# Transposing x in blocks of 16 rows by two neighbouring columns instead of whole columns

## The reference, cut to what matters

```python
def _L0_conv_ref(x, p1, p3, p4, p5, p6):
    t1 = jnp.einsum('nchw,he->ncew', x, p1)            # p1: (32, 16), sums over the rows h
    t2 = three row-shifted copies of x
    t3 = conv(t1, p3, 9x9, one filter per channel)
    t4 = conv(t3, p4, 5x1, groups of 4 channels)
    t5 = jnp.einsum('ncew,ewf->ncf', t4, p5[:, :, 0, :])
    t6 = conv(t5, p6, 3 taps along f)
    return einsum('ncf,nfp->ncp', t6, t2) / sqrt(3 * c)
...
    x = x + _L0_conv_ref(_gn(x), ...)
    x = x + _L1_conv_ref(_gn(x), conv_w, gamma, beta)
```

## Time and profile before

| | us |
|---|---|
| median of 3 runs | 307.37 |
| lowest and highest | 307.35, 309.02 |
| the profiled execution | 308.8 |
| its span | 307.0 |

### The profile page before, as it was taken

The page is one execution under the profiler, slowest core; times in us unless marked ns, Lnnn a source line. Parts: engine busy times, 40 slices in busy tenths (PEclk is TensorE's granted clock), DMA queues, the critical chain, the costliest instruction groups (busy, mean ns, idle before and its releaser), DMA issues.

```text
span 307.0 us, 6666 instructions
## 1 busy us (share of the span) xinstructions
PE 251.1 (82%) x2662; PEld 192.6 (63%) x2662; DVE 237.2 (77%) x479; ACT 200.8 (65%) x268; POOL 164.5 (54%) x186
## 2 busy tenths in 40 slices
PE   6899978998775599899999999999999998850000
PEld 3333345665645397789998899888998887630000
DVE  2899996044564767778999999998999987866992
ACT  1788722277539254764878778787787777465990
POOL 4000001987605721578888898888988889540000
PEclk9999999999969599999999999999999999995555
DMA  7996041666710700000000000000000000000798
GB/s 218 410 410 227 0 125 38 177 179 173 235 63 2 275 0 0 2 0 2 1 0 2 1 0 0 3 0 2 0 0 2 2 0 3 0 0 20 316 403 355
DMA packets 11487, 28.00 MB, mean 91 GB/s; under 512 B 2528, under 2 KB 3616, under 8 KB 11456
## 3 DMA queue, kind: packets, MB, share of 16 engines
q1 hardware_dynamic: 8624, 21.37, 19.3%
q10 hardware_dynamic: 1232, 4.46, 3.9%
q0 software_dynamic: 1600, 1.74, 2.3%
HBM read 16.39 MB, written 8.39 MB: 81 GB/s over the span
## 4 chain that ended last, share of the span: by engine, by line
PE 70%; DVE 10%; issue 6%; POOL 4%; ACT 4%; DMA 3%; SPq 0%; DVEq 0%; POOLq 0%
PE low L618 10%; PE low L230 9%; PE high L594 8%; PE low L232 8%; PE low L231 8%; DVE x_sb L972 5%; PE high L729 4%; PE high L230 4%; PE high L232 4%; PE high L231 4%; PE high L632 3%; DMA x_sb<-in_x 3%; PE high L733 3%; DVE d_split L793 2%; POOL g_lo L401 2%
## 5 line engine op out<-in xcount | busy, mean ns | idle before, releaser
L264 POOL DMA_DIRECT2D d_st<-t_sb x50 | 24.7, 502 | 52.7 <-ACT t_sb L455 52.4
L401 POOL TENSOR_TENSOR g_lo<-y_sb,g_hi 128x1024 fp32r<-128x1024 f32 x15 | 36.1, 2409 | 14.4 <-ACT y_sb L550 14.4
L377 POOL TENSOR_TENSOR g_lo<-y_sb,g_hi 128x1024 fp32r<-128x1024 f32 x15 | 35.9, 2390 | 10.2 <-ACT g_hi L510 10.2
L230 PE MATMUL low<-g_hi,t_hi 128*128 128x512 f32 x96 | 37.6, 391 | 0.7 <-DVE t_lo L892 0.7
L232 PE MATMUL low<-g_hi,t_lo 128*128 128x512 f32 x96 | 37.5, 390 | 0.0
L231 PE MATMUL low<-g_lo,t_hi 128*128 128x512 f32 x96 | 37.4, 389 | 0.0
L793 DVE TENSOR_TENSOR d_split<-d_st,d_split 128x272 fp32r<-128x272 f32 x20 | 16.1, 873 | 26.0 <-ACT d_split L467 26.0
L549 ACT ACTIVATE g_hi<-x_sb,rs 128x1024 fp32r<-128x1024 f32 x16 | 21.3, 1334 | 19.6 <-POOL rs L386 19.6
L784 DVE STREAM_TRANSPOSE xa<-x_sb 128x1024 f32<-128x1024 f32 x15 | 28.1, 1951 | 6.8 <-DMA x_sb<-in_x 6.8
L594 PE MATMUL high<-xa,p_blk 128*128 128x512 f32 x64 | 29.9, 617 | 1.0 <-DVE xa L784 1.0
L618 PE MATMUL low<-t_all,taps 32*32 32x272 f32 (+1 forms) x960 | 24.4, 407 | 6.9 <-issue 6.6
(11 more groups left out here) (136 smaller groups left out, 679.3 us busy)
## 6 DMA issues: line engine op xcount, KB each, us to landing
out<-x_sb SPq DMA_DIRECT2D x6, 1024.0 KB, 4.9
x_sb<-in_x SPq DMA_DIRECT2D x11, 512.0 KB, 10.3
x_sb<-in_x ACTq DMA_DIRECT2D x8, 512.0 KB, 12.6
taps<-in_taps SPq DMA_DIRECT2D x6, 320.0 KB, 4.1
d_st<-t_sb POOLq DMA_DIRECT2D x50, 34.0 KB, 2.5
mix<-in_mix SPq DMA_DIRECT2D x6, 256.0 KB, 4.6
out<-x_sb SPq DMA_DIRECT2D x3, 512.0 KB, 3.2
d_st<-t_sb SPq DMA_DIRECT2D x30, 34.0 KB, 3.1
```

What stands on the lines that cost most here:

```text
L230: nc.tensor.matmul(ps, w[0], m[0], start=start, stop=False)
L264: eng.dma_start(d_st[32 * jl:32 * jl + 32, r % DR, co].rearrange("p b k -> p (b k)"), t4_sb[32 * co:32 * co + 32, r % 2, jl].rearrange("p ...
L377: pool.tensor_tensor(g1_lo[:, W:W + HW], y_sb[:, n, :], g1_hi[:, W:W + HW].bitcast(F32), ALU.subtract).then_inc(s["g1_lo"], 1)
L401: pool.tensor_tensor(g2_lo[:, :], y_sb[:, n, :], g2_hi[:, :].bitcast(F32), ALU.subtract).then_inc(s["g2_lo"], 1)
```

## The change

VectorE transposes each image in two halves, hh = 0 for the upper 16 rows of the image and hh = 1 for the lower 16. Inside a half a block of 32 elements is no longer a column of 32 rows, but 16 rows (k) by two neighbouring columns (v): the source is read as "p (k j v) -> p j k v", two words side by side and then a hop of 128 bytes. After the transposition the partitions of a block hold (k, v), and xa's dimensions are half, column pair j and channel. It is written contiguously, as before.

TensorE's two products of an image are then the two halves of h, added in PSUM, in place of even and odd columns. Each reads 512 contiguous elements of a partition and each waits for its own half (`2 * i - 1 + hh`). The table p1_blk keeps its size and is filled on the host for the new order of the partitions. The output in PSUM is the same, and so is all that follows.

```diff
-        xa = put("xa", [XR, W, G])
+        xa = put("xa", [XR, 2, J, G])
...
-                if i >= 1:
-                    pe.wait_ge(s["xa"], i)
                 if i >= 4:
                     pe.wait_ge(s["t1_hi"], i - 3)
-                for v in range(2):
-                    if i == N and v:
-                        pe.wait_ge(s["xa"], i + 1)
-                    rhs, ps = (xa[:, (i - 1) % XR, v:W:2, :], ps_t1[i % 4]) if i else (ones_row[:, 0:G], ps_t1[0][:, 0:G])
-                    mm = pe.matmul(ps, p1_blk[:, v, :], rhs, start=(v == 0), stop=(v == 1))
+                for hh in range(2):
+                    if i >= 1:
+                        pe.wait_ge(s["xa"], 2 * i - 1 + hh)
+                    rhs, ps = (xa[:, (i - 1) % XR, hh], ps_t1[i % 4]) if i else (ones_row[:, 0:G], ps_t1[0][:, 0:G])
+                    mm = pe.matmul(ps, p1_blk[:, hh, :], rhs, start=(hh == 0), stop=(hh == 1))
                 mm.then_inc(s["t1_mm"], 1)
...
                 if n >= XR:
                     dve.wait_ge(s["t1_mm"], n - XR + 2)
-                columns = x_sb[:, n, :].rearrange("p (h w) -> p w h", w=W)
-                if n < N - 1:
-                    dve.transpose(xa[:, n % XR], columns).then_inc(s["xa"], 1)
-                    continue
-                for v in range(2):
-                    dve.transpose(xa[:, n % XR, v:W:2, :], columns[:, v:W:2, :]).then_inc(s["xa"], 1)
+                for hh in range(2):
+                    rows = x_sb[:, n, HALF * hh:HALF * hh + HALF].rearrange("p (k j v) -> p j k v", j=J, v=2)
+                    dve.transpose(xa[:, n % XR, hh], rows).then_inc(s["xa"], 1)
...
-    p1_blk = np.zeros((B, H, 2, B, 2, E), np.float32)
+    p1_blk = np.zeros((B, H // 2, 2, 2, B, 2, E), np.float32)
     for b in range(B):
         for v in range(2):
-            p1_blk[b, :, v, b, v, :] = L0_conv_p1
+            p1_blk[b, :, v, :, b, v, :] = np.asarray(L0_conv_p1).reshape(2, H // 2, E).transpose(1, 0, 2)
```

## The result

| | median us | lowest to highest | runs |
|---|---|---|---|
| before | 308.03 | 306.31 to 312.04 | 22 |
| the change | 306.98 | 304.42 to 308.73 | 22 |

The ratio is 0.995, 95% interval 0.9928 to 0.9972: the change is faster by 1.5 us (0.9 to 2.2); the two medians in the table differ by 1.05 us, which is within that. Forecast were 3.0 us and 304.4. The forecast took its 2.96 us off a median of three runs, 307.37; over 22 runs before has 308.03, so 0.66 us of the distance between 304.4 and 306.98 is that starting point. The profiled execution of the change took 305.81 us with a span of 304.1, 3 us under that of before; that is only one pair of executions, and the executions of either kernel scatter over more than 4 us.

The account below looks back on a forecast made before the run. VectorE's transpositions were taken to bound the stage making t1, TensorE right behind. 1.26 us from an earlier start plus 1.70 from the pace, 2.96 in all, off the median 307.37 gave 304.4 us, range 303.3 to 306.8.

Parts of the forecast that it names:

- VectorE is the bound of the stage, TensorE right behind it: Stage making t1: VectorE's transpositions set the pace, 1.87 us an image; TensorE goes at 1.86 and could go at 1.72.
- The hop at every element is the cost, and pairs take it away: VectorE's transposition: reading two words side by side brings a half from 0.95 to 0.60 us, with latency 0.70.
- 1.26 us from the start and 1.70 from the pace: Products of t1: image 2 starts 1.26 us earlier, the 14 images from there take 1.70 less; sum 2.96 us.
- Taps 2 goes out at 35.5; it wasn't late and isn't now: SP's load of taps 2 goes out at about 35.5 instead of 41.47, in time for its use at 51.4.
- The rounds are a chain that moves with TensorE, so the 2.96 us should reach the end: Eight rounds after the stage: they start from TensorE and return to it, so the whole 2.96 us is kept.
- if the convolution is 3 us earlier and the end is not: One of the prediction's signs of being wrong: first convolution 3 us earlier without the kernel's end following.
- given back behind the stage: Rival, chance 0.10: instructions late behind the earlier loads of taps 2 and mix 2 cost 2.1 us, giving 306.5.
- the loads are as large as before and in the same convolution: First convolution: argument against late instructions, since loads of taps 2 and mix 2 keep their size and fall within it.
- The other argument, 26 us of products beside the loads of x without such a wait: Stage before the first convolution: second argument against late instructions; its products ran beside loads without an issue wait.
- The waits called "issue": Convolutions from 38 to 103 us: TensorE's largest waits, 6.6 us in seven, longest 2.1, without a cause in the trace.

Follow-up runs that it names:

- e3: The kernel before with every image transposed in two halves, single words read as before, and a wait for each product; ratio to before 1.001.
- e14: The changed kernel run a third time with no edit; ratio to before 0.9944.
- e1: The changed kernel run a second time with no edit; ratio to before 0.9949.
- e9: The changed kernel, but both products of an image wait for its second half; ratio to before 0.9954.
- e10: The changed kernel with one small product (four instructions) added in TensorE's idle time before p1_blk lands; ratio to before 0.9974.
- e12: The kernel before, additionally loading the tables of taps 2 and mix 2 into xa's free buffers when the products end; ratio to before 1.0034.
- e8: The changed kernel with image 0 loaded once more (512 KB) ahead of taps 2; ratio to before 0.9949.

## Why the prediction failed

- *VectorE is the bound of the stage, TensorE right behind it*: right. A half at 0.95 us (e3) gives products until 38.6, one at 0.63 or less until 35.2.
- *The hop at every element is the cost, and pairs take it away*: right. Forecast 0.60 us in pitch and 0.70 in latency; 5.41 to 5.41 + 2.49 for four is (2.49 - 0.67) / 3 = 0.61 in pitch, the mean latency 0.68. The rule of the Trainium skill that one source hopping at every element costs 1.73 ns an element and runs of two adjacent words keep the full rate (Vector Engine (DVE) Microarchitecture Reference, 5.2) holds here for the transposition too, which its table doesn't list: 1.71 with single words, and in pairs a half has the pace of a bn_stats on 512 contiguous elements, 0.61 against 0.60 us.
- *1.26 us from the start and 1.70 from the pace*: the products ended 3.16 us sooner against 2.96 forecast. 1.43 came from the start (image 2's first record at 11.10 instead of 12.53) and 1.73 from the pace. That the start gave more is luck of the execution: image 2 landed at 10.31 instead of 10.50.
- *Taps 2 goes out at 35.5; it wasn't late and isn't now*: the time was right to the digit and the conclusion too narrow. I asked whether the load is in time for its user, not what else is on the queues when it runs. This is the step that failed: the 1 us and more that the load at 35.5 takes from TensorE's instructions was put at nothing in the sum.
- *The rounds are a chain that moves with TensorE, so the 2.96 us should reach the end*: wrong. The first convolution takes 5.08 to 5.24 us in the three profiles of the change and 4.25 in before, so it gives back 0.8 to 1.0 us (over all versions: 5.01 to 5.52 in the seven profiles with a load in front of the fetch, 4.10 to 4.25 in the four without). In the change's profile 1.96 us of 3.15 are left behind the second convolution, within the 0.9 to 2.2 that was timed. The prediction named the sign itself, "if the convolution is 3 us earlier and the end is not", and it came. The rival "given back behind the stage" named this mechanism, late instructions behind loads, with 2.1 us and a chance of 0.10. Its size was too large and its chance too small; what I held against it was that the loads are as large as before and in the same convolution. But 2.5 us into it the fetch had already landed (39.87 + 1.30 = 41.17, the load 41.47), and at its start it had not. The other argument, 26 us of products beside the loads of x without such a wait, says nothing: no packet of TensorE's instructions was fetched in those 26 us, the first in the span is the one at 39.87, and by the prediction's own count the loads of x had landed by 25.8.
- The waits called "issue" were called without a cause. For those in the first two convolutions the DMA view had it: each 16 KB packet on the instruction queue, the first one 0.95 us into the first convolution.
- Between the 2.0 us left behind the second convolution and the 1.5 timed may lie the later waits of the same kind, which scatter: the sixth convolution starts 1.4, 1.7 and 2.4 us sooner than before's 69.74 in the three profiles of the change. The runs can't split that half microsecond.

## What to carry to other kernels

Where a stage gets faster, list the DMAs that its engines had been holding back, and look at what else needs the queues at the new time, TensorE's own instructions included. Before a stretch of many small matmuls, look in the DMA view for the first 16 KB packet of instructions: if it starts behind the stretch's beginning, a few instructions more in an idle stretch may put it ahead, and a large load belongs behind it. For VectorE, order a strided read so that two neighbouring words come together (0.61 us a half here in place of 0.95), and split the product to suit.

## What the runs showed that I had not expected

- Twelve instructions of no use, in a stretch where TensorE was idle, took 4 us off the change (0.982 against 0.995 of before), and twenty took 2.6 us off the kernel before. The Trainium skill (Runtime: NRT & Kernel Launch, Instruction fetch mechanics) says that instructions come in blocks of 256 and that crossing a block's end is mostly hidden. The 16 KB packets agree. The rest doesn't hold here: a convolution of 80 products of 32 x 32, 320 instructions with the weight loads, took 3.41 us (some 90 instructions per microsecond) with the fetch ahead, 4.1 to 4.25 with it 1 us behind, and 5.0 to 5.5 with a load in front of it.
- TensorE's granted clock fell in the change where it had not in before. After 0.66 us of work in the three us from 39 to 42 it was granted 1.2 GHz, half of full speed:

```profile
39.00:42.00 3.00, 0.66 (x21) 1.00 0.02 5
42.00:44.00 2.00, 1.78 (x65) 0.50 0.60 172
```

  (stretch, length, PE busy and instructions, granted clock, DMA share, GB/s). Conv 1, the second convolution, then took 5.29 us in one piece; at full clock in e14 it took 5.02, of which 1.00 was a wait called issue beside the next fetch. So the lower clock costs 0.3 us there and hides behind that wait otherwise. It fell at about 42 us in e1, e9 and e10 too, at 45 in e12, and not in e14 and e8. e8 had the longer pauses (1.56 and 1.27 us against 1.29 and 1.27) and the same 0.65 us of work from 39 to 42, so what decides it is open.
